# A decoder layer on one core: gate products placed behind the first projections, cross-attention keys and values a slot later over two pairs of banks

## The reference

```python
x = x + attn(layernorm(x))             # gated delta rule, 16 heads, keys of 128, values of 256
x = x + xattn(layernorm(x), ctx, mask) # cross-attention, 16 heads of 8 channels over the 128 rows
x = x + ffn(layernorm(x))              # shared expert and top 2 of 8 experts, in bf16
```

```python
state = state * at
err = vt - einsum('bhkv,bhk->bhv', state, kt)
state = state + bt * einsum('bhk,bhv->bhkv', kt, err)
ot = einsum('bhkv,bhk->bhv', state, qt)
```

## Time and profile before

| | us |
|---|---|
| median of 3 runs | 937.96 |
| lowest, highest | 933.4, 1081.68 |
| profiled execution | 934.79 |
| its span, first to last instruction | 932.9 |
| TensorE busy (matmul) | 828.1 |
| VectorE busy | 719.7 |
| ScalarE busy | 617.8 |
| GpSimd busy | 540.2 |

### The profile page before, as it was taken

One profiled execution on the slowest core, in us unless ns is written; L12 is line 12 of the kernel. 1 busy time (PEld: TensorE's weight loads), 2 busy tenths in 40 slices (PEclk: granted clock), 3 DMA queues, 4 the chain that ended last, 5 costly groups with the idle time before them and its releaser, 6 DMA issues.

```text
span 932.9 us, 21903 instructions
## 1 busy us (share of the span) xinstructions
PE 828.1 (89%) x7371; PEld 531.5 (57%) x7408; DVE 719.7 (77%) x1227; ACT 617.8 (66%) x1022; POOL 540.2 (58%) x689
## 2 busy tenths in 40 slices
PE   3578999999999999999999999998867898889997
PEld 2245776677667766777677767765543333323353
DVE  7768888888888888887888788884556756674746
ACT  3377887788778877887888778873230565567522
POOL 6439769678696796886966968574302232322300
PEclk9989999999999999999999999999985777778999
DMA  6202010010110100101101000000001500000000
GB/s 194 57 1 80 1 35 27 11 35 0 34 34 0 34 19 15 34 0 34 34 0 34 10 23 11 2 2 1 1 1 27 94 15 18 16 14 25 10 23 24
DMA packets 34416, 23.98 MB, mean 26 GB/s; under 512 B 5062, under 2 KB 33414, under 8 KB 34235
## 3 DMA queue, kind: packets, MB, share of 16 engines
q1 hardware_dynamic: 31643, 19.00, 7.2%
q0 software_dynamic: 2720, 4.29, 2.2%
HBM read 22.68 MB, written 1.05 MB: 25 GB/s over the span
## 4 chain that ended last, share of the span: by engine, by line
PE 66%; DVE 17%; issue 9%; ACT 5%; POOL 2%; DVEq 1%; DMA 0%; SPq 0%; ACTq 0%; POOLq 0%
PE psum L1294 13%; PE psum L1310 11%; PE psum L1474 6%; DVE y L1004 6%; PE psum L1619 3%; PE psum L1571 3%; PE psum L1364 3%; PE psum L1354 3%; DVE mx L1138 3%; DVE ux L984 3%; PE psum L1382 2%; PE psum L1503 2%; PE psum L1389 1%; PE psum L1392 1%; PE psum L1708 1%
## 5 line engine op out<-in xcount | busy, mean ns | idle before, releaser
L1004 DVE SCALAR_TENSOR_TENSOR y<-psum,cwh,y 128x508 f32<-128x508 f32 (+2 forms) x384 | 281.5, 740 | 18.4 <-ACT y L697 12.4
L491 POOL TENSOR_TENSOR ct<-lm,levels 128x256 f16<-128x256 f32 x224 | 152.0, 701 | 18.4 <-DVE lm L1027 18.4
L477 POOL TENSOR_TENSOR sql<-sq,sqh 128x1024 f16<-128x1024 f32 x32 | 68.4, 2137 | 126.3 <-ACT sq L744 126.3
L697 ACT ACTIVATE y<-psum,cwh 128x512 f32<-128x512 f32 x128 | 99.4, 777 | 50.8 <-PE psum L1294 50.8
L1310 PE MATMUL psum<-wo,vt 128*128 128x256 f32 x512 | 126.0, 389 | 1.2 <-DVE y L1004 1.0
L1310 PEld LDWEIGHTS psum<-wo,vt 128*128 128x128 f32 x512 | 92.3, 190 | 11.9 <-DVE y L1004 2.0
L817 ACT ACTIVATE et<-psum 128x1024 f32<-128x1024 f32 x64 | 65.2, 1022 | 43.3 <-PE psum L1605 43.3
L1138 DVE TENSOR_REDUCE mx<-psum 128x4 f32<-128x1024 f32 x64 | 77.2, 1219 | 21.4 <-PE psum L1584 21.3
L1294 PE MATMUL psum<-xth,whi 128*128 128x512 f16 x256 | 78.0, 387 | 8.7 <-DVE y L1004 5.4
L984 DVE TENSOR_TENSOR ux<-ux,psum 128x512 f16<-128x512 f16 x64 | 43.9, 686 | 53.8 <-PE psum L1392 52.7
L1294 PE MATMUL psum<-xth,wlo 128*128 128x512 f16 x256 | 78.0, 387 | 0.0
(11 more groups left out here) (215 smaller groups left out, 2016.6 us busy)
## 6 DMA issues: line engine op xcount, KB each, us to landing
wraw<-in_L_attn_Wv SPq DMA_DIRECT2D x32, 128.0 KB, 2.7
wo<-in_L_attn_Wo SPq DMA_DIRECT2D x16, 256.0 KB, 2.8
wraw<-in_L_attn_Wk SPq DMA_DIRECT2D x16, 128.0 KB, 2.5
wraw<-in_L_attn_Wq SPq DMA_DIRECT2D x16, 128.0 KB, 2.7
moved<-avs SPq DMA_DIRECT2D x128, 16.0 KB, 1.8
x<-in_x SPq DMA_DIRECT2D x8, 128.0 KB, 4.1
maskrow<-in_mask_row POOLq DMA_DIRECT2D x1, 1024.0 KB, 4.5
xt<-in_ctx SPq DMA_DIRECT2D x1, 1024.0 KB, 6.1
```

Source lines behind the costliest of these rows:

```text
L477: g.tensor_tensor(lo, f, hi, ALU.subtract).then_inc(sq_split, 1)
L491: g.tensor_tensor(dst, src, pick.unsqueeze(1).to_broadcast([P, NB, T // (2 * m), m]), ALU.mult).then_inc(masked[l], 1)
L697: s.activation(y[:, n], ubank[n % 2].rearrange("p (j t) -> p j t", j=NB), ACT.Identity, scale=cwh[:, (a.c // 2) % 2, n, TAPS - 1:TAPS], bi ...
L1004: v.scalar_tensor_tensor(out=y[:, n, :, sh:], in0=u[:, :, 0:T - sh], scalar=cwh[:, (a.c // 2) % 2, n, TAPS - 1 - sh:TAPS - sh], in1=y[:, n ...
```

## The change

The gates' products, sums and VectorE's part of them move from before the loop into slot -2: the products behind the second projection, the copy behind the taps of tile 1, the activations behind the bias of tile 1, the sums behind the fourth projection. Norms of slot -1 wait for the gates instead. Projections of slots -2 and -1 wait for the four or eight `xtl` that they read. `bias5` is prepared at the end of slot -1, `mask5` at the end of slot 0. GpSimd splits head 0 before it issues the eight DMAs, and without the wait for `xn`; each x tile gets a semaphore of its own; ScalarE loads one table set ahead of its first activation; the turned x goes through banks 4 and 5.

Keys and values move from slots 30 and 31 to slots 31 and 32. Batches alternate between banks 0, 1 and banks 2, 3 (`kbank`). The value products of a batch are issued behind the key products of the next, and VectorE's additions behind its stacking. The mask and bias rows lie in `vv` instead of `zz`. The wait of z in slot 31 for values is gone.

```diff
-        zrow = zz[0:5].rearrange("p r j n -> p (r j n)")
+        zrow = vv[0:5].rearrange("p b s n -> p (b s n)")
...
+        kbank = (ubank, ebank)
...
-                sp.dma_start(x1[:, b, :], x_in[:, b, :]).then_inc(x_loaded, 16)
+                sp.dma_start(x1[:, b, :], x_in[:, b, :]).then_inc(x_loaded[b], 16)
...
-            for dst, src in ((maskrow[:], d["mask_row"].partition_broadcast(P)),
-                             (wks[:], d["xk"]), (wvt[:], d["xv"]), (stackcol[:], d["stackcol"]), (biasf, d["xbias"]),
-                             (bvrow[:], d["bv_row"].partition_broadcast(P)), (maskcol[:], d["mask_col"]), (wqs[:], d["xq"])):
-                g.dma_start(dst, src).then_inc(xattn_loaded, 16)
...
             pool.wait_ge(conv_scaled, 3)
-            pool.wait_ge(xn_done, B)
             split(0, 0, None)
+            for dst, src in ((maskrow[:], d["mask_row"].partition_broadcast(P)),
+                             (wks[:], d["xk"]), (wvt[:], d["xv"]), (stackcol[:], d["stackcol"]), (biasf, d["xbias"]),
+                             (bvrow[:], d["bv_row"].partition_broadcast(P)), (maskcol[:], d["mask_col"]), (wqs[:], d["xq"])):
+                g.dma_start(dst, src).then_inc(xattn_loaded, 16)
...
+            s.preload_act_table_set("natural_log_exp_and_others")
             norm_act(act, 0, slice(0, B))
...
+                s.activation(xt[:, :, b * T:(b + 1) * T], quad[:, b % 2, 0:H].rearrange("p (c t) -> p c t", c=CH), ACT.Copy).then_inc(xt_full, 1)
...
+                def gate_act_():
+                    if k.i is None and k.c == -2:
+                        act.wait_ge(gate_step, 1)
+                        s.activation(ga[:], gz[:], ACT.Abs).then_inc(gate_act, 1)
+                        act.wait_ge(gate_act, 1)
+                        s.activation(ga[:], ga[:], ACT.Exp, scale=-1.0).then_inc(gate_act, 1)
+                        act.wait_ge(gate_act, 2)
+                        s.activation(ga[:], ga[:], ACT.Ln, bias=1.0).then_inc(gate_act, 1)
...
-                    if k.i is None and k.c in (STEPS - 2, STEPS - 1):
-                        bb = (k.c - STEPS + 2) * 4 + n
+                    if k.i is None and k.c in (STEPS - 1, STEPS):
+                        bb = (k.c - STEPS + 1) * 4 + n
...
+                            s.activation(kh[:, 1 - m], kbank[bb % 2][1 - m], ACT.Copy).then_inc(k_high, 1)
...
                 bias(1)
+                gate_act_()
                 k_split(1)
...
-                    dve.wait_ge(x_loaded, 16 * B)
+                    dve.wait_ge(x_loaded[b], 16)
...
-            dve.wait_ge(gate_psum, 1)
-            v.tensor_copy(gz[:], bank[2][:, 0:B * 2 * HK]).then_inc(gate_step, 1)
-            dve.wait_ge(xattn_loaded, 16 * 8)
-            dve.wait_ge(mask_cast, 1)
-            v.tensor_copy(mask5[0:4], maskrow[0:4]).then_inc(mask_cast, 1)
-            v.tensor_copy(biash, biasf).then_inc(bias_cast, 1)
-            dve.wait_ge(gate_act, 3)
-            dve.wait_ge(gate_step, 1)
-            v.scalar_tensor_tensor(out=gl[:].rearrange("p b n -> p (b n)"), in0=gz[:], scalar=0.0, in1=ga[:], op0=ALU.min, op1=ALU.subtract).then_inc(gate_step, 1)
-            dve.wait_ge(cum_psum, 1)
-            v.tensor_copy(gcum[:].rearrange("p h b -> p b h"), bank[3][:, 0:B * HK].rearrange("p (b h) -> p b h", b=B)).then_inc(gates_done, 1)
-            dve.wait_ge(gates_done, 1)
-            dve.wait_ge(gate_step, 2)
-            v.tensor_tensor(gcol[:].rearrange("p h b -> p b h"), gl[:, :, HK:], gcum[:].rearrange("p h b -> p b h"), ALU.subtract).then_inc(gates_done, 1)
-            dve.wait_ge(mask_cast, 2)
-            m5 = mask5[0:4].rearrange("p b n -> p (b n)")
-            v.scalar_tensor_tensor(out=m5, in0=m5, scalar=stackcol[0:4, 3:4], in1=maskrow[0:4].rearrange("p b n -> p (b n)"), op0=ALU.mult, op1=ALU.add).then_inc(mask_ready, 1)
-            dve.wait_ge(bias_cast, 1)
-            v.tensor_copy(bias5[:], biash).then_inc(bias_cast, 1)
-            dve.wait_ge(bias_cast, 2)
-            v.scalar_tensor_tensor(out=bias5[0:4].rearrange("p k g n -> p (k g n)"), in0=biash[0:4].rearrange("p k g n -> p (k g n)"),
-                                   scalar=stackcol[0:4, 2:3], in1=biasf[0:4].rearrange("p k g n -> p (k g n)"), op0=ALU.mult, op1=ALU.add).then_inc(bias_ready, 1)
...
+                def gate_raw():
+                    if k.i is None and k.c == -2:
+                        dve.wait_ge(gate_psum, 1)
+                        v.tensor_copy(gz[:], bank[2][:, 0:B * 2 * HK]).then_inc(gate_step, 1)
+                def gate_sums():
+                    if k.i is None and k.c == -2:
+                        dve.wait_ge(gate_act, 3)
+                        dve.wait_ge(gate_step, 1)
+                        v.scalar_tensor_tensor(out=gl[:].rearrange("p b n -> p (b n)"), in0=gz[:], scalar=0.0, in1=ga[:], op0=ALU.min, op1=ALU.subtract).then_inc(gate_step, 1)
+                        dve.wait_ge(cum_psum, 1)
+                        v.tensor_copy(gcum[:].rearrange("p h b -> p b h"), bank[3][:, 0:B * HK].rearrange("p (b h) -> p b h", b=B)).then_inc(gates_done, 1)
+                        dve.wait_ge(gates_done, 1)
+                        dve.wait_ge(gate_step, 2)
+                        v.tensor_tensor(gcol[:].rearrange("p h b -> p b h"), gl[:, :, HK:], gcum[:].rearrange("p h b -> p b h"), ALU.subtract).then_inc(gates_done, 1)
+                def prepare_bias():
+                    if k.i is None and k.c == -1:
+                        dve.wait_ge(xattn_loaded, 16 * 8)
+                        v.tensor_copy(biash, biasf).then_inc(bias_cast, 1)
+                        dve.wait_ge(bias_cast, 1)
+                        v.tensor_copy(bias5[:], biash).then_inc(bias_cast, 1)
+                        dve.wait_ge(bias_cast, 2)
+                        v.scalar_tensor_tensor(out=bias5[0:4].rearrange("p k g n -> p (k g n)"), in0=biash[0:4].rearrange("p k g n -> p (k g n)"),
+                                               scalar=stackcol[0:4, 2:3], in1=biasf[0:4].rearrange("p k g n -> p (k g n)"), op0=ALU.mult, op1=ALU.add).then_inc(bias_ready, 1)
+                def prepare_mask():
+                    if k.i is None and k.c == 0:
+                        dve.wait_ge(xattn_loaded, 16 * 8)
+                        dve.wait_ge(mask_cast, 1)
+                        v.tensor_copy(mask5[0:4], maskrow[0:4]).then_inc(mask_cast, 1)
+                        dve.wait_ge(mask_cast, 2)
+                        m5 = mask5[0:4].rearrange("p b n -> p (b n)")
+                        v.scalar_tensor_tensor(out=m5, in0=m5, scalar=stackcol[0:4, 3:4], in1=maskrow[0:4].rearrange("p b n -> p (b n)"), op0=ALU.mult, op1=ALU.add).then_inc(mask_ready, 1)
...
+                        v.scalar_tensor_tensor(out=vv[:, bb, st], in0=bvrow[:], scalar=maskcol[:, bb, st:st + 1], in1=kbank[bb % 2][0][:, st * P:(st + 1) * P],
...
-                    if not (k.i is None and k.c in (STEPS - 2, STEPS - 1)):
-                        return
-                    bb = (k.c - STEPS + 2) * 4 + n
-                    if n > 0:
-                        v_add(bb - 1)
+                    if not (k.i is None and k.c in (STEPS - 1, STEPS)):
+                        return
+                    bb = (k.c - STEPS + 1) * 4 + n
...
+                                               in1=kbank[bb % 2][hh], op0=ALU.mult, op1=ALU.add).then_inc(k_stack, 1)
+                    if n > 0:
+                        v_add(bb - 1)
...
+                gate_raw()
...
+                gate_sums()
...
-                if k.i is None and k.c in (STEPS - 2, STEPS - 1):
-                    v_add((k.c - STEPS + 2) * 4 + 3)
+                if k.i is None and k.c in (STEPS - 1, STEPS):
+                    v_add((k.c - STEPS + 1) * 4 + 3)
...
+                prepare_bias()
+                prepare_mask()
...
+                    mm = t.transpose(quad[:, b % 2, c * P:(c + 1) * P], xn[:, b, c * P:(c + 1) * P], ident[:])
...
-            for b in range(B):
-                pe.wait_ge(xt_full, b + 1)
-                for c in range(CH):
-                    mm = t.matmul(bank[2][:, b * 2 * HK:(b + 1) * 2 * HK], xt[:, c, b * T:(b + 1) * T], wab[:, c, :], start=(c == 0), stop=(c == CH - 1))
-            mm.then_inc(gate_psum, 1)
-            pe.wait_ge(gate_step, 2)
-            t.matmul(bank[3][:, 0:B * HK], tri[:], gl[:, :, 0:HK], start=True, stop=True).then_inc(cum_psum, 1)
-            pe.wait_ge(xt_low, B)
-            pe.wait_ge(gates_done, 2)
...
+                    if k.i is None and k.c in (-2, -1):
+                        pe.wait_ge(xt_low, (k.c + 3) * NB)
...
+                def gate_products():
...
+                    if k.i is None and k.c == -2:
+                        for b in range(B):
+                            pe.wait_ge(xt_full, b + 1)
+                            for c in range(CH):
```

(39 more changed lines are left out.)

16 lines of the change are left out of this document (3 added, 13 removed).

## The result

The kernel after takes 928.83 us (median of 20 runs, 926.46 to 935.58); the kernel before took 936.2 in as many runs of the same days. Three executions of before, at 993 us and above, are in the slow state and left out of the ratio of the two, which is 0.9933 with a 95% interval of 0.991 to 0.9955: about 6 us faster, less than 1%. The profiled execution took 927.6 us (span 925.7), 7.2 us less than that of before; forecast were 922.1 and 12.7 us less.

A forecast was written before the change was run, and what follows sets the result against it. The prediction took TensorE's stream and its waits to bound the kernel: 934.8 us less 6.6 at the start, 4.6 at the end and 1.5 for first q products gave 922.1, range 914 to 931.

The forecast's parts named there:

- The first projection: Start of the kernel: TensorE's first projection would start at 20.2 us instead of 32.93.
- Slots 30 and 31: End of the loop: 12.0 us gained in slot 30 without its batches, 1.9 in slot 31 from fewer waits for keys.
- The wait behind GpSimd's masking: Slot 30: TensorE idles some 4 us before 633.63 and then runs at a lower clock; charged 2.0 us.
- The last output products: Behind slot 32: they would take 1.89 us instead of 3.78 because the clock stays up, 1.9 us saved.
- The gate products: Start, behind two projections: 32 products from 25.4 to 30.5, between their old 6.9 us and half of it.
- The preparations: Ends of slots -1 and 0: bias and mask work on VectorE would give back 1.8 and 1.7 us.
- Slot 32 +9.3: End of the loop: four key and value batches added to slot 32 would lose 9.3 us net.
- they keep the clock up: Slot 32: the added batches would hold TensorE's clock up, saving 1.9 us on output products and about 1.9 on others.
- Rival 5: Slot 30's idle stretch drops the clock and it stays down: slower, up to 50 us lost; chance 0.05.
- the queries' first steps: Behind the loop: some first q products would run at the full clock right behind dense work, 1.5 us gained.
- Rival 2: The end gives nothing, batches being moved, not removed, and slot 30 at half clock: 928 or 931 us; chance 0.2.
- Rival 4: The start gives half: weights land late or the preparations cost 3.0 and 3.2 us: 925 to 930; chance 0.08.

The follow-up runs named there:

- one_pair: The kernel after with keys and values over one pair of banks and values ahead of the next keys; 939.6 us, ratio 1.003 to the kernel before.
- after_again: The kernel after, unchanged, profiled a second time; slots 30 to 32 took 21.3, 27.4 and 31.8 us, first q product at 701.4.
- prep_in_gaps: The kernel after with the bias prepared mid slot -1 and the mask in slot 30, where VectorE idles; 924.1 us, ratio 0.991 to the kernel before.
- filler_all: The kernel after with eighteen products of no use put into five waits of slot 32; 924.5 us, ratio 0.987 to the kernel before.
- keys_in_waits: The kernel after with bias, mask and context masking moved into idle gaps and three half key batches into slot 32's waits; 910.0 us, ratio 0.973 to before.
- before_again: The kernel before, unchanged, profiled a second time; first q product at 703.9, 226.6 us from there to the end.
- start_alone: The kernel before with only the new start; keys and values stay in slots 30 and 31 over one bank pair; 933.8 us, ratio 1.000 to before.
- end_alone: The kernel before with only the new end: keys and values in slots 31 and 32 over two bank pairs; 936.3 us, ratio 1.002 to before.

## Why the prediction was right and wrong

**What held.** The first projection at 20.2; to the digit by luck, since GpSimd's split ended at 19.44 (forecast 19.8) and the projection then waited for VectorE's `xtl`. Slots 30 and 31: 13.6 and 2.0 us gained for 12.0 and 1.9 (slot 30 alone scatters by 1.5), and one_pair shows that the second pair of banks with its order of products is what does it in slot 31. The wait behind GpSimd's masking and a low clock behind it, charged with 2.0 us. The last output products at the full rate. Which operations would stand in front of `lm`.

**The gate products.** Charged with 5.1 us (25.4 to 30.5), between two prices; they took 3.65, the full rate, behind projections that had reached 0.59 us a pair. That is 1.45 of the 2.4 us by which the norms of slot -1 came earlier than forecast; 1.0 more is the two projections in front, whose clock had risen by 23.5. (The forecast's own chain also adds up to 40.5, not 40.3.) The rule weighed there, from the Trainium skill, TensorE: Matmul & The Clock Gate, Part 1, was the better guide for this term: by it the norms would have been 11.7 us earlier, and they were 12.5.

**The preparations: right mechanism, size wrong.** Charged 1.8 and 1.7 us; from z to z slot 0 lost 3.9 (2.5 in after_again) and slot 1 5.0 (5.2), 8.9 together for 3.5: 5.4 us too little. Three things were missing. The casts wait for GpSimd too: 2.40 and 2.99 us, against 0.67 and 1.2 in prep_in_gaps; the prediction had weighed this and left it out of the sum because no row showed it. The 1.83 us of idle of the earlier trace rows was taken as cover for the mask; from z to z slot 1 lost 5.0 us for 5.3 us of preparation, so nothing was covered: what follows waits for the norms, which wait for the same multiplication. And while TensorE waited, its clock fell, at 57 and at 78, and the next projections ran at 1.06 us a pair instead of 0.59; in after_again it did not fall at 57, which is the 1.4 us between 3.9 and 2.5.

**Slot 32: the step that failed.** "Slot 32 +9.3", output products of slot 33 included, rested on "they keep the clock up". Measured were 18.6 lost in slot 32 and 1.9 gained in slot 33: 16.7, so 7.4 us too little. filler_all has the same batches in the same order with the clock up: 25.1 us for slot 32, 11.9 more than before, and 1.9 back in slot 33. Its filler (3.8 us) is 0.5 us longer than the waits that it fills (3.3), so the batches cost an estimated 9.5 in all; keys_in_waits, with useful work in the waits, comes to 8.0. So the work was priced rightly, and the whole of the 7.4 is the assumption on the clock. (With the shortest spell that an unchanged slot 32 had, 29.6 us, it would still be 5.2.) Rival 5 had a falling clock, but with slot 30's idle stretch as its cause and all dense work behind as its price. The real cause is smaller and nearer: waits of 0.78, 0.48 and 0.78 us in the head of slot 32, and two more of 0.78 and 0.47 behind them. Before has such waits too, and its clock falls behind the first three (0.51 from 690 on), but with light work behind. The change put the estimated 16 us of dense work behind those waits instead of into them.

**What nobody had on the list.** The stretch behind the first q product took 224.2 us against 229.0. About 1.0 of it is the queries' first steps, partly at the full rate, for 1.5 forecast: from the first q product to the first maxima took 7.87 us against 8.86. This part repeats: it took 8.86 in all four profiles with the end of before and 7.1 to 8.0 in the thirteen with batches in slot 32. The rest goes with the clock: over seventeen profiles the stretch takes 223.2 to 230.4 us, and its mean granted clock is 0.84 in the two shortest, 0.80 in the longest, 0.82 in after and 0.81 in before (0.82 in before_again, 226.6 us). Whether this change has a part in that, and what share of the 6 us between the kernels comes from there, stays open.

**The sum.** 6.6+4.6+1.5 = 12.7 forecast; 3.6-1.2+4.8 = 7.2 found in the profile. That the time lies as near to the forecast as it does is in part luck: 4.8 of the 7.2 us are the last term, most of which is the clock in a stretch that the change leaves alone. Rival 2 (the end gives nothing) had the end right, 928, for another reason than it gave: half clock in slot 32, not in slot 30. Rival 4 (the start gives half) had the start right, with preparations that cost more than even its 3.0 and 3.2. What stands before the first q product, 2.4 us for 11.2 forecast, is both of them together.

## What to carry to other kernels

Before moving dense work behind a stretch of light work, look at the waits in that stretch: here five waits of under a microsecond each put 10 to 17 us at half clock, and three half batches of key products placed into those waits instead of behind them made that slot 6.5 us shorter (29.6 to 23.1). Work on a small tile that goes "to the end of a slot" stands in front of the first instruction of the next; put it behind the last one that another engine waits for, where its own engine waits and GpSimd does nothing. And with a clock that falls in spells, halves of a change do not add up: compare the marks slot by slot, look how far the same slot scatters in kernels that leave it alone, and profile a kernel twice before believing a difference of 5 us in one slot.

## What the runs showed of the hardware

VectorE and GpSimd delay each other both ways, by nearly the whole length of the overlap: a cast of 5x1024 took 2.40 us beside a subtraction of GpSimd that it found running, and 0.67 without; a subtraction of 2.13 us took 4.16 beside a scalar-tensor-tensor operation of 4x2048 that was there first; eight multiplications of 5.68 us in all took 8.79 beside 3.9 us of such work, while VectorE's cast among them took its usual 1.2.

A low spell of TensorE's clock does not end as soon as the engine is dense: in before it lasted 3.5 us in slot 30, in start_alone 14, in after 17 in slot 32, the last 10 of them with TensorE busy throughout. Where it begins and how long it lasts differs between profiles with the same instructions and waits: 17, 14 or 10 us in slot 32, 10 us or none in slot 31 of end_alone. The Trainium skill, TensorE: Matmul & The Clock Gate, Part 1, says that the chip looks at the engine's activity at times of its own, which do not start with the kernel's work. The two profiles of end_alone would fit that, with the same waits 0.45 us apart and the lower clock in one of them only; the two of start_alone, 2.3 us apart with the same spell, neither show it nor speak against it.
